# A two-layer graph network kernel: in the second layer, one 512-column matmul per tile of a sum in place of two of 258 and 256

## The reference

```
def _scatter_mean(src, row, num_segments):
    sums = segment_sum(src, row)
    cnt = segment_sum(ones, row)
    return sums / maximum(cnt, 1.0)[:, None]

h = maximum(layernorm(x), 0)
z = h
for l in range(2):
    weights = softmax(z @ envW[l] + envb[l])            # N x 4
    agg = _scatter_mean(z[col], row, N)
    combined = concatenate([agg, z], axis=-1)           # N x 512
    outputs = einsum('nd,kdo->nko', combined, W[l]) + z[:, None, :]
    z = relu(einsum('nk,nko->no', weights, outputs))
return x + z
```

## Time and profile before

| | us |
|---|---|
| median of 3 runs | 1840.04 (1839.89 to 1840.95) |
| span of the profiled execution, first to last instruction | 1839.2 |
| TensorE busy in it | 1598.5 (87%) |
| TensorE weight loads | 1124.8 (61%) |
| VectorE | 895.0 (49%) |
| ScalarE | 572.7 (31%) |
| GpSimd | 1214.2 (66%) |

### The profile page before, as it was taken

How to read it: one execution, slowest core, us unless ns; L and a number is a source line. 1 busy time by engine, 2 the same in 40 slices (tenths; PEclk the granted TensorE clock), 3 DMA queues, 4 the chain that set the end, 5 groups by cost and what they waited for, 6 DMA issues and landing times. The chain is left out here.

```text
span 1839.2 us, 36146 instructions
## 1 busy us (share of the span) xinstructions
PE 1598.5 (87%) x8502; PEld 1124.8 (61%) x8503; DVE 895.0 (49%) x2024; ACT 572.7 (31%) x1254; POOL 1214.2 (66%) x1187
## 2 busy tenths in 40 slices
PE   1059999999999999999998389999999999999998
PEld 1036665666666666666665266666666666667665
DVE  6665565655565565555564224334443333443333
ACT  4414333334434333433333022222222222222222
POOL 1377776766776676676663677666666666666764
PEclk9989999999999999999999599999999999999999
DMA  7877766666666666666656987677777777777775
GB/s 218 284 216 227 215 206 186 189 180 195 206 191 197 193 175 194 205 195 197 193 173 215 382 259 244 214 221 220 220 221 222 220 220 220 219 216 215 225 219 150
DMA packets 160202, 393.34 MB, mean 214 GB/s; under 512 B 36989, under 2 KB 61080, under 8 KB 160180
## 3 DMA queue, kind: packets, MB, share of 16 engines
q0 software_dynamic: 92544, 302.70, 55.2%
q10 hardware_dynamic: 35112, 61.46, 9.4%
q1 hardware_dynamic: 32524, 28.91, 5.1%
HBM read 347.61 MB, written 45.37 MB: 214 GB/s over the span
## 5 line engine op out<-in xcount | busy, mean ns | idle before, releaser
L713 POOL DMA_INDIRECT ring<-zp_dram,gather_idx x1152 | 1196.1, 1038 | 535.8 <-issue 271.6
L1333 PE MATMUL agg_ps<-zp,stage 128*128 128x258 f32 x1568 | 447.3, 322 | 23.6 <-PEq L101 23.6
L1366 PE MATMUL mix_ps<-w_sb,turned_m 128*128 128x512 f32 x784 | 405.4, 617 | 16.0 <-PEq L101 14.8
L1295 PE MATMUL agg_ps<-ring,onehot 128*128 x1248 | 398.5, 346 | 23.8 <-PEq L101 17.0
L1366 PE MATMUL mix_ps<-w_sb,turned_z 128*128 128x512 f32 x784 | 400.9, 611 | 10.8 <-PEq L101 10.8
L1335 PE MATMUL agg_ps<-zp,stage 128*128 128x256 f32 x1568 | 384.6, 281 | 0.0
L1075 ACT ACTIVATE stage<-counts_sb 128x512 fp32r<-128x512 uint8 (+1 forms) x416 | 247.1, 605 | 387.5 <-ACTq L101 386.6
L1333 PEld LDWEIGHTS agg_ps<-zp,stage 128*128 128x128 f32 x1568 | 296.1, 189 | 87.7 <-issue 83.9
L1300 PE MATMUL agg_ps<-ring,onehot 128*128 x1248 | 328.2, 289 | 0.0
L1335 PEld LDWEIGHTS agg_ps<-zp,stage 128*128 128x128 f32 x1568 | 296.4, 189 | 34.5 <-issue 34.5
L1295 PEld LDWEIGHTS agg_ps<-ring,onehot 128*128 128x128 f32 x1248 | 242.7, 194 | 79.2 <-issue 73.1
(11 more groups left out here) (157 smaller groups left out, 944.4 us busy)
## 6 DMA issues: line engine op xcount, KB each, us to landing
ring<-zp_dram,gather_idx POOLq DMA_INDIRECT x1152, 3.8
zp_dram<-zp SPq DMA_DIRECT2D x7, 1792.0 KB, 7.3
a_dram<-counts_sb ACTq DMA_DIRECT2D x16, 784.0 KB, 4.9
zp_dram<-parts ACTq DMA_DIRECT2D x49, 256.0 KB
zp<-zp_dram SPq DMA_DIRECT2D x4, 1792.0 KB, 16.3
counts_sb<-a_dram ACTq DMA_DIRECT2D x17, 400.0 KB, 6.4
parts<-in_x ACTq DMA_DIRECT2D x48, 128.0 KB
counts_sb<-a_dram ACTq DMA_DIRECT2D x16, 384.0 KB, 5.4
```

Of the source, the lines that this page charges most:

```text
L713: pool.indirect_dma_start(out=ring[:, k, t, 0:2 * D].bitcast(F32), out_offset=None, in_=zp_dram[l], in_offset=bass.IndirectOffsetOnAxis(ap ...
L1295: mm = pe.matmul(agg_ps[:, bank, 0:D + 2], onehot[:, place, t, :], rows[:, :, D:2 * D + 2], start=place == 0 and t == 0, stop=True, skip_g ...
L1333: pe.matmul(agg_ps[:, bank, 0:D + 2], stage[:, g % 2, i, :], zp[:, c, D:2 * D + 2], start=c == 0, stop=True, skip_group_check=True)
L1366: mm = pe.matmul(mix_ps[i][:, :], (turned_z, turned_m)[what][:, c, :], w[:, i * HALF:(i + 1) * HALF], start=what == 0 and c == 0, stop=wha ...
```

## The change

In the second layer a tile of a sum is one matmul of 512 columns into a whole bank, with the low parts' sum in columns 256 to 511. VectorE makes the mean from both halves: the old operation on the high half, and a second that multiplies the low half by `rcnt` and adds the first's result. The second waits for the first. The first layer, which needs the count, stays as it was. Two dummy matmuls, which only signal, now write into `lg_ps`, since the bank that they wrote to has no free columns any more.

```
@@ take_mean
-                        nc.vector.tensor_scalar(mean[:], agg_ps[:, bank, 0:D], rcnt[:, bass.ds(blk, 1)], None,
-                                                ALU.mult).then_inc(s_mean, 1)
+                        if l == 0:
+                            nc.vector.tensor_scalar(mean[:], agg_ps[:, bank, 0:D], rcnt[:, bass.ds(blk, 1)], None,
+                                                    ALU.mult).then_inc(s_mean, 1)
+                        else:
+                            settle(nc.vector.tensor_scalar(mean[:], agg_ps[:, bank, 0:D], rcnt[:, bass.ds(blk, 1)],
+                                                           None, ALU.mult))
+                            nc.vector.scalar_tensor_tensor(out=mean[:], in0=agg_ps[:, bank, D:2 * D],
+                                                           scalar=rcnt[:, bass.ds(blk, 1)], in1=mean[:],
+                                                           op0=ALU.mult, op1=ALU.add).then_inc(s_mean, 1)
@@ add
-                            mm = pe.matmul(agg_ps[:, bank, 0:D + 2], onehot[:, place, t, :],
-                                           rows[:, :, D:2 * D + 2], start=place == 0 and t == 0, stop=True,
-                                           skip_group_check=True)
+                            begins = place == 0 and t == 0
+                            if l == 0:
+                                mm = pe.matmul(agg_ps[:, bank, 0:D + 2], onehot[:, place, t, :],
+                                               rows[:, :, D:2 * D + 2], start=begins, stop=True,
+                                               skip_group_check=True)
+                            else:
+                                mm = pe.matmul(agg_ps[:, bank, :], onehot[:, place, t, :], rows[:, :, 0:2 * D],
+                                               start=begins, stop=True, skip_group_check=True)
...
-                            mm = pe.matmul(agg_ps[:, bank, 0:D], onehot[:, place, t, :], rows[:, :, 0:D],
-                                           start=False, stop=True, skip_group_check=True)
+                            if l == 0:
+                                mm = pe.matmul(agg_ps[:, bank, 0:D], onehot[:, place, t, :], rows[:, :, 0:D],
+                                               start=False, stop=True, skip_group_check=True)
@@ group_sum: the same, with stage[:, g % 2, i, :] and zp[:, c, ...]
@@ more_units, and the start of a layer
-                                pe.matmul(agg_ps[:, bank, 2 * P + P:], ident[:], ident[:], start=False, stop=True,
+                                pe.matmul(lg_ps[:, 2 * P:3 * P], ident[:], ident[:], start=False, stop=True,
```

More of the change, by code:

```diff
@@ L1332, in group_sum @@
                             c = g * STAGE + i
[L1333 to L1336, removed]
+                            if l == 0:
+                                pe.matmul(agg_ps[:, bank, 0:D + 2], stage[:, g % 2, i, :], zp[:, c, D:2 * D + 2],
+                                          start=c == 0, stop=True, skip_group_check=True)
+                                mm = pe.matmul(agg_ps[:, bank, 0:D], stage[:, g % 2, i, :], zp[:, c, 0:D],
+                                               start=False, stop=True, skip_group_check=True)
+                            else:
+                                mm = pe.matmul(agg_ps[:, bank, :], stage[:, g % 2, i, :], zp[:, c, 0:2 * D],
+                                               start=c == 0, stop=True, skip_group_check=True)
                         mm.then_inc(s_sfree, 1)
@@ L1518, in _ @@
                         more_units(l, head, 0)
-                        pe.matmul(agg_ps[:, 0, 2 * P + P:], ident[:], ident[:], start=False, stop=True,
+                        pe.matmul(lg_ps[:, 2 * P:3 * P], ident[:], ident[:], start=False, stop=True,
                                   skip_group_check=True).then_inc(s_agg, 1)
```

## The result

| | before | changed |
|---|---|---|
| median of 4 runs, us | 1839.97 (1838.01 to 1840.95) | 1853.44 (1853.13 to 1855.75) |
| ratio, 95% interval | | 1.0075 (1.0062 to 1.0087) |
| span of the profiled execution, us | 1839.2 | 1853.9 (its own time 1855.75) |
| TensorE busy, us | 1598.5 | 1596.4 |
| VectorE busy, us | 895.0 | 918.5 |

I had forecast 1840.6, with a range up to 1850, and the most likely outcome was "no change one can tell". It is a clear loss, and outside the range.

A forecast was written before the change was run, and what follows sets the result against it. Second-layer chains from VectorE's mean through ScalarE were taken to bound most of the round, TensorE's speed only the rest. TensorE's 23.6 us gain against the second operation's 24.3 us cost gave +0.7, 1840.6 us, range 1837 to 1850.

The forecast's parts named there:

- The three chains with the mean at their head: Second layer: VectorE's mean starts three paths through ScalarE that TensorE waits for; a second operation there costs 24.3 us.
- gathers that don't bind: GpSimd's gathers were said not to limit the round: GpSimd waits 86.7 us for free room in `ring`.
- B: Path from product 5 to group 2 of the dense slot; the second mean operation adds 0.64 us a round.
- C: Path from the dense slot's product 6 to the rest slot's product 4; the second operation adds 0.26 us.
- A: Path from the rest slot's product 6 to the next round's product 4; the second operation adds 0.64 us.
- The tile: TensorE's sums: a tile falls from 0.2364 to 0.2163 us, 1.15 us a round over 57 dense-slot tiles.
- rival 1: Tile gains less: fixed price per matmul stays, 1848.5 us, chance 0.12; or cost goes with columns, 1859, chance 0.05.
- The late starts: Unit 1, after the wait for group 2: TensorE falls behind its cadence; 0.22 us a round counted as won.
- the wait at group 9: Group 9 waits for its half of `stage`; the wait grows from 0.10 to 0.2 us, a loss of 0.10.
- the dense stretch: TensorE from group 2 to product 6 of the dense slot, 16.89 us, to get 1.37 us shorter a round.
- the first slot's gain: Product 4 to product 5 of the first slot, 4 tiles: 0.10 us a round shorter, 1.5 us in all.
- The clock: Rival: longer waits at the first slot's product 4 lower TensorE's granted clock, giving 1848 us; chance 0.07.

The follow-up runs named there:

- e1: Changed kernel with one operation for the mean, so the wide matmuls alone, low parts left out of the mean: 1832.04 us, 0.9946 of before.
- e2: Kernel before plus a second, waited operation of the same size in the second layer's mean, without wide matmuls: 1862.87 us, 1.0112 of before.
- e5: Kernel before with VectorE's second-layer order changed, result ahead of compare_first (first slot) and compare_more (round's end): 1811.53 us, 0.9839 of before.
- e8: Kernel before with an extra waited VectorE operation behind result in the first and dense slots, not the rest slot: 1840.17 us, 1.0000 of before.
- e4: Changed kernel with bursts of fp32r and bf16 matmuls of several widths behind its last product, to time them: 1882.56 us, a single run.
- e3: Changed kernel with each 512-column matmul cut into two of 256 columns, into separate halves of the bank: 1863.05 us, 1.0116 of before.
- e7: Kernel before with an extra waited VectorE operation behind result in every slot of the second layer: 1856.27 us, 1.0084 of before.
- e6: Changed kernel with VectorE's second-layer order changed, result ahead of compare_first and compare_more: 1817.45 us, 0.9867 of before.

## Why the prediction was wrong

- **The bound.** Right. The three chains with the mean at their head, the places where TensorE is fast in vain, and gathers that don't bind: e1, e2, e5 and e8 agree to a few tenths of a microsecond a round.
- **The mean's price on the chains.** Right for B (0.63 for 0.64) and C (0.27 for 0.26). On A 0.44 came of 0.64, because ScalarE's loop head took 0.2 us less.
- **The tile, "I take 512 / 2.4 + 0.003 = 0.2163 us, a gain of 0.0201 per tile".** This is the step that failed. The tile went to 0.233, from 0.238 on average, a gain of 0.005: 57 tiles give 0.3 us a round and not 1.15. This was nearly the lesser half of rival 1, that the cost goes with the columns, which I gave 0.05. Two rows had led me to it, the fp32 products and the bf16 matmuls, and neither is of the tiles' type at full pace. An fp32 product runs at half the pace, 0.43 us for 512 columns, where a limit of 0.447 ns per column can't be seen, and bf16 turned out to be the faster type. What makes fp32r slower no run shows. In the kernel before only two fp32r widths occur, 256 and 258, and through one width any number of lines can be drawn: fixed price, load of weights, or price per column. I weighed these by rows of another type, where an honest weighing was that none of the rows told them apart. The Trainium skill's page "TensorE: Matmul & The Clock Gate" ("Back-to-back issue gap") would have had nearly no gain per tile, which is what came. Its figure for 256 columns, 0.109 us, is not what e4 measured for this type, 0.119, and for 512 it is 0.216 against 0.233: the measurement decides both, and the gain came out small because both are larger by about the same share. For bf16 e4 measured 0.109 and 0.216, so there the trace agrees. The upper end of the gain in the forecast, 0.0207 with no fixed price at all, was also worked out wrongly: 0.2364 - 512 / 2.4 GHz is 0.0231. Nothing hung on it.
- **The late starts and the wait at group 9.** About right: the rest of the dense stretch's gain, 0.2 us, is what I had counted for them (-0.22 - 0.10 + 0.10). The late starts behave as I had read them: units 0 and 1 behind group 2 take 1.17 us in the kernel before and 1.15 in e3, but 0.96 in e5, where no wait stands ahead of group 2, and 0.93 in the changed kernel, where a tile is one matmul.
- **The sum.** With 0.3 in place of 1.15 for the tiles the forecast would have been 0.85 x 16 = 13.6 us higher, 1854.2, against 1853.4 measured. That it comes so near is in part luck: chain A cost 3 us less than counted (15 x 0.2), and the first slot's gain of 1.5 us was mostly missing, as was any term for the second layer's start, which came 2.5 us later in the profiled execution.
- **The clock** stayed at 1.00 from 1117 us on; product 4 of the first slot was waited for 1.10 to 1.36 us, less than the 1.6 to 1.9 of the forecast, since TensorE's work before it hardly got shorter.

## What to carry to other kernels

When a step is priced from rows of another type or pace, keep the whole span between "no gain" and "full gain" in the range and in the chances: here both ends stood in the text, and the untested one of 5% nearly came true. Look for what stands first on each chain that ends a wait: one VectorE operation of 0.5 us, with a wait ahead of it, at the head of three chains cost 21 us, the same kind of operation twice a round behind them nothing, and moving matrices that nothing was waiting for behind the result won 29. And the end of a loop's body can stand on a chain of the next round, as e7 shows.

## What was not expected of the hardware

- At a granted clock of 1.00 an fp32r matmul of 512 columns takes 0.456 ns per column, all in, and a bf16 one 0.421. Between 256 and 512 columns fp32r costs 0.447 ns per column and 0.004 us per matmul; a load of weights doesn't show.
- ScalarE's way around its loop, from the store of a result to the load of `x`, takes 2.58 us in one kernel, 2.37 in another and 2.55 in e6. The kernels differ by shifts of a few tenths of a microsecond on other engines; what decides is not shown.
- A waited operation of 0.48 us at the end of VectorE's loop body costs 2.05 us (e7). Where it stands inside the body the kernel's time stays the same (e8).
